# A start-up sequence written out for one step more, with a new order of work on every engine, in a 16-graph attention kernel

## The chip, the cores and the metric

The kernel runs on one core of a Trainium2 chip. The metric is the device time of one execution in microseconds (us). TensorE is called PE, VectorE DVE, ScalarE ACT, GpSimd POOL, and the queue that issues most plain loads and stores SP.

## What is computed

For 16 graphs of 512 nodes with 256 features each, two layers run one after the other, each with a residual and a layer norm:

```python
# layer 0: graph attention
h = x @ W_fc.T;  f1 = h @ a1;  f2 = h @ a2
scores = leaky_relu(f1[:, :, None] + f2[:, None, :], 0.2)
scores = where(adj == 0, -1e9, scores)
h_prime = softmax(scores, axis=2) @ x
x = layernorm(x + elu(h_prime))
# layer 1: similarity, adjacency, features
xn = x / sqrt(max(sum(x * x), 1e-12))
out = ((xn @ xn.T) @ adj) @ x
x = layernorm(x + out)
```

## The kernel before

One graph is one unit of work `g`; its 512 rows are four chunks `c` of 128 partitions, and the 256 features are two halves `d`. Nothing is planned at run time: each engine has one list of calls, written out by hand, and runs it strictly in that order. Semaphores tie the lists together. So the order inside each list, and nothing else, sets what waits for what.

A step on PE, in the names of the code: `transpose_prob(g, c)` (L1117) turns a softmax block; `attend(g, c)` (L1137 for graphs 0 and 1, L1140 to L1142 from graph 2 on, 12 matmuls a call) multiplies it with x; `make_z(g, c)` (L1170, L1171, 8 matmuls) multiplies the adjacency with the normalised xn; `transpose_xn(g, d)` (L1182); `make_w(g, d)` (L1200 to L1202, 12 matmuls); `make_out(g, c)` (L1214, 4 matmul records); `bcast_f2(g)` (L1106) spreads the column scores. Three PSUM banks `ps_l1` are used in turn by z, xnT, w and out; `bank_free` lets PE write a bank once the reader of the tile three places earlier is done.

ACT does, per graph: `make_mask` (L783), `lrelu` (L793), `softmax_exp` (L804), `probT_hi_part` (L813), `elu_exp` (L824), `elu_relu` (L830), `xn_hi_part` (L838), `scale_z` (L857), `copy_xnT` (L866), `copy_w` (L872) and `normalise2` (L890, four activations). DVE does `node_scores` (L433), `masked_f2` (L449), `negate_max`, `denominators`, `probT_lo_part` (L486), `residual` (L494), `row_moments` (L527, L531), `normalise` (L540), `z_lo_part` (L549), `residual2` (L560) and `row_moments2` (L590). POOL does `residual_sum` (L278), `shifted_moments` and `power` (L285 to L295), `norm`, `split_xn` (L311), `split_x` (L267), `shifted_moments2`, `power2` (L340), `shift2` (L347), and issues the loads `load_adj` (L259) and `load_x_hi` (L252). SP issues `load_x` and `store`.

The steps are skewed: step `i` of the loops attends graph `i`, makes z and w of graph `i - 1`, makes the output of graph `i - 2`, and prepares the softmax of graph `i + 1`. Each list has a head written out call by call, a loop `for i in range(3, B - 2)` with one steady order (B is 16), and a tail written out again. The lists in the head differ from the order of the loop, since the pipeline is filling.

Two chains matter later. For xn: `elu_relu(g, 3)` on ACT, `residual(g)` on DVE, `residual_sum(g)` on POOL, `row_moments(g)` on DVE, `shifted_moments(g)` and `power(g)` on POOL, `normalise(g)` on DVE, `xn_hi_part(g)` on ACT, `split_xn(g)` on POOL, then `make_z(g, 0)` on PE. For the output: `make_out(g, 0)` waits for `copy_xnT(g, 0)`, `copy_xnT(g, 1)`, `copy_w(g, 0)` and `copy_w(g, 1)`, all on ACT. And `attend(g, c)` for c of 2 or more waits for `elu_relu(g, c - 2)`, which frees its PSUM bank.

## Time and profile before

| | |
|---|---|
| median of 3 runs | 336.14 us (335.92 to 337.16) |
| the profiled execution | 337.11 us |
| its span, first to last instruction | 335.2 us |
| PE busy | 320.5 us (96%) |
| ACT busy | 291.2 us (87%) |
| DVE busy | 282.6 us (84%) |
| POOL busy | 206.2 us (62%) |
| mean granted TensorE clock | 0.991 of full speed |
| moved by DMA | 41.38 MB, mean 123 GB/s |

The profiled execution is 1.9 us longer than its span (what lies before the first and after the last instruction), and 0.97 us above the median of the runs. Busy time says how much of the span an engine worked; starts and ends in the rows are in us from the start of the span. Matmuls overlap in the pipeline, so one call's cost is read from start to start, not from the length of a row. A line beginning with an engine name in a list of waits tells who waited, for whom, for how long in all, how often, and the longest.

### The profile page before, as it was taken

Reading aid. Unit: us, or ns where it says so; the run is one execution under the profiler, and the core shown is the slowest. Engines: PE = TensorE matmul, PEld = TensorE weight load, DVE = VectorE, ACT = ScalarE, POOL = GpSimd, SP = SyncE. Lnnn points to the kernel's source line nnn. Section 1 sums busy time; section 2 is a strip of 40 time slices with the busy share of each in tenths; the row PEclk is TensorE's granted clock in tenths of the full one; section 3 lists DMA queues with packets and bytes.
Section 4 is the critical chain, followed back from the end, with each engine's and each line's share of the span. In section 5 each row is a group of like instructions: output and inputs, shape, how many; then the busy total and the mean of one; then the engine's idle time right before and its main releaser. Section 6 shows DMA issues by size and latency. Waiting matters only on the chain.

```text
span 335.2 us, 7276 instructions
## 1 busy us (share of the span) xinstructions
PE 320.5 (96%) x2376; PEld 301.4 (90%) x2376; DVE 282.6 (84%) x1000; ACT 291.2 (87%) x606; POOL 206.2 (62%) x236
## 2 busy tenths in 40 slices
PE   8998999997979999999999999999999999999992
PEld 5777999997979999999999999999999999998881
DVE  4899998897498989899898989899898988947635
ACT  4988889998399999999999999999999998993561
POOL 4044775856058576666858576666858576665623
PEclk9999999999899999999999999999999999999998
DMA  7774506215224554462554564553653551210121
GB/s 221 221 188 129 165 26 177 81 59 186 69 63 127 151 162 128 114 192 74 172 143 126 153 163 127 123 183 74 175 142 126 150 165 65 64 65 0 49 78 63
DMA packets 32964, 41.38 MB, mean 123 GB/s; under 512 B 1152, under 2 KB 24736, under 8 KB 32928
## 3 DMA queue, kind: packets, MB, share of 16 engines
q0 software_dynamic: 15888, 24.12, 26.5%
q1 hardware_dynamic: 16992, 16.81, 16.0%
q8 instruction: 19, 0.31, 0.4%
q14 instruction: 17, 0.14, 0.1%
q10 hardware_dynamic: 48, 0.00, 0.0%
HBM read 32.54 MB, written 8.39 MB: 122 GB/s over the span
## 4 chain that ended last, share of the span: by engine, by line
PE 86%; DVE 6%; ACT 4%; issue 2%; POOL 1%; POOLq 0%; DVEq 0%; ACTq 0%
PE ps_l L1214 16%; PE ps_l L1170 9%; PE ps_l L1171 8%; PE ps_h L1140 8%; PE ps_probT L1117 8%; PE ps_h L1141 8%; PE ps_h L1142 8%; PE ps_l L1200 4%; PE ps_l L1202 4%; PE ps_l L1201 4%; PE ps_l L1182 4%; PE ps_h L1137 3%; PE ps_f L1106 2%; DVE product L433 1%; PE ps_l L1197 1%
## 5 line engine op out<-in xcount | busy, mean ns | idle before, releaser
L1140 PE MATMUL ps_h<-x_hi,probT_hi 128*128 128x256 f32 x224 | 69.0, 308 | 0.7 <-issue 0.7
L1170 PE MATMUL ps_l<-xn_hi,adj_sb 128*128 128x256 f32 x256 | 63.9, 288 | 2.8 <-POOL xn_lo L311 1.7
L1214 PE MATMUL ps_l<-w_sb,xnT 128*128 128x256 f32 x256 | 63.1, 383 | 2.2 <-ACT xnT L866 1.9
L1141 PE MATMUL ps_h<-x_lo,probT_hi 128*128 128x256 f32 x224 | 63.0, 281 | 0.0
L1142 PE MATMUL ps_h<-x_hi,probT_lo 128*128 128x256 f32 x224 | 62.9, 281 | 0.0
L1171 PE MATMUL ps_l<-xn_lo,adj_sb 128*128 128x256 f32 x256 | 62.5, 283 | 0.0
L311 POOL TENSOR_TENSOR xn_lo<-xn,xn_hi 128x1024 fp32r<-128x1024 f32 x15 | 36.0, 2401 | 41.0 <-ACT xn_hi L838 41.0
L1170 PEld LDWEIGHTS ps_l<-xn_hi,adj_sb 128*128 128x128 f32 x256 | 48.9, 191 | 4.5 <-DVE y L560 2.7
L1214 PEld LDWEIGHTS ps_l<-w_sb,xnT 128*128 128x128 f32 x256 | 45.5, 190 | 8.0 <-ACT xnT L866 2.2
L1171 PEld LDWEIGHTS ps_l<-xn_lo,adj_sb 128*128 128x128 f32 x256 | 48.9, 191 | 0.0
L433 DVE CUSTOM_DVE_ANT_0 product<-x_sb,v_bcast 128x256 bf16<-128x256 f32 x128 | 47.1, 426 | 0.0
L804 ACT ACTIVATE prob<-score,neg_max 128x512 f32<-128x512 f32 x64 | 46.5, 728 | 0.2
L793 ACT ACTIVATE score<-score,f 128x512 f32<-128x512 f32 x64 | 44.4, 723 | 2.1 <-DVE row_max L449 2.1
L1140 PEld LDWEIGHTS ps_h<-x_hi,probT_hi 128*128 128x128 f32 x224 | 42.7, 191 | 3.8 <-DVE probT_lo L486 1.9
L449 DVE CUSTOM_DVE_ANT_0 score<-mask,ps_f 128x512 f32<-128x512 bf16 x64 | 41.3, 685 | 3.7 <-ACT mask L783 3.6
L1141 PEld LDWEIGHTS ps_h<-x_lo,probT_hi 128*128 128x128 f32 x224 | 42.7, 191 | 0.7
L278 POOL TENSOR_TENSOR y<-y,exp_h 128x1024 f32<-128x1024 f32 x15 | 36.1, 2408 | 11.1 <-DVE exp_h L494 10.8
L1142 PEld LDWEIGHTS ps_h<-x_hi,probT_lo 128*128 128x128 f32 x224 | 42.6, 190 | 0.0
L486 DVE TENSOR_TENSOR probT_lo<-ps_probT,probT_hi 128x512 fp32r<-128x512 f32 x56 | 36.9, 680 | 2.4 <-ACT probT_hi L813 2.4
L1117 PE MATMUL ps_probT<-ident,prob 128*128 128x128 f32 x256 | 38.0, 273 | 0.4 <-ACT prob L804 0.2
L560 DVE SCALAR_TENSOR_TENSOR y<-xn,nrm,ps_l 128x256 f32<-128x256 f32 x64 | 29.4, 477 | 9.8 <-PE ps_l L1214 9.5
L857 ACT ACTIVATE z_hi<-ps_l,nrm 128x256 fp32r<-128x256 f32 x60 | 28.3, 473 | 10.4 <-PE ps_l L1171 8.9
(82 smaller groups left out, 819.9 us busy)
## 6 DMA issues: line engine op xcount, KB each, us to landing
adj_sb<-adj POOLq DMA_DIRECT2D x15, 1024.0 KB, 5.9
x_sb<-x SPq DMA_DIRECT2D x16, 512.0 KB, 4.6
out<-o_sb SPq DMA_DIRECT2D x15, 512.0 KB, 3.2
x_hi<-x POOLq DMA_DIRECT2D x14, 512.0 KB, 4.1
adj_sb<-adj POOLq DMA_DIRECT2D x4, 256.0 KB, 4.8
out<-o_sb SPq DMA_DIRECT2D x4, 128.0 KB, 1.7
wfc<-w_fc SPq DMA_DIRECT2D x1, 32.0 KB, 2.0
attn_cols<-w_attn ACTq DMA_DIRECT2D x1, 0.2 KB, 1.7
```

Source lines behind the costliest of these rows:

```text
L433: last = nc.vector.tensor_tensor_reduce(out=product[:, k, c, :], in0=x_sb[n][:, c, :], in1=v_bcast[:, k, :], scale=1.0, scalar=0.0, op0=AL ...
L449: nc.vector.tensor_tensor_reduce(out=score[:, c, :], in0=mask[:, c, :], in1=ps_f2[:], scale=1.0, scalar=LOWEST, op0=ALU.add, op1=ALU.max, ...
L486: nc.vector.tensor_tensor(probT_lo[:, c, :], ps_probT[c % 2][:], probT_hi[:, c, :].bitcast(F32), ALU.subtract).then_inc(probT_ok, 1)
L793: nc.scalar.activation(score[:, c, :], score[:, c, :], ACT.Prelu, bias=f[n][:, 0, c:c + 1], scale=1.0, alpha=SLOPE).then_inc(lrelu_ok, 1)
L804: nc.scalar.activation(prob[:, c, :], score[:, c, :], ACT.Exp, bias=neg_max[n][:, c:c + 1], scale=1.0, accum_out=den[n][:, c:c + 1]).then_ ...
L1117: last = nc.tensor.transpose(ps_probT[c % 2][:, k * P:(k + 1) * P], prob[:, c, k * P:(k + 1) * P], ident[:])
L1140: nc.tensor.matmul(ps, probT_hi[:, c, blk], x_hi[n][:, k, :], start=(k == 0), stop=False)
L1141: nc.tensor.matmul(ps, probT_hi[:, c, blk], x_lo[n][:, k, :], start=False, stop=False)
L1142: last = nc.tensor.matmul(ps, probT_lo[:, c, blk], x_hi[n][:, k, :], start=False, stop=(k == NC - 1))
L1170: nc.tensor.matmul(ps, a, xn_hi[n][:, k, :], start=(k == 0), stop=False)
L1171: last = nc.tensor.matmul(ps, a, xn_lo[n][:, k, :], start=False, stop=(k == NC - 1))
L1214: last = nc.tensor.matmul(ps, xnT[:, d, c * P:(c + 1) * P], w_sb[:, d, :], start=(d == 0), stop=(d == DC - 1))
```

## The change

Every list gets one more step written out before its loop, and the loops start at 4 in place of 3. The body of the loops and the tails are not touched. Each call that was made before is made once again, so each engine has the same instructions in another order. Within the head the order is new on DVE, ACT, PE and POOL, from the first graph on, most of it by one to ten places; SP loads x of graph 5 before it stores graph 0, and POOL issues `load_x_hi` for graphs 3, 4 and 5 earlier. The diff, without the reordering of DVE's and ACT's lists for the first two graphs:

```diff
--- before.py
+++ after.py
@@ -221,8 +221,10 @@
             load_x(2)
             load_x(3)
             load_x(4)
+            load_x(5)
             store(0)
-            for i in range(3, B - 2):
+            store(1)
+            for i in range(4, B - 2):
                 load_x(i + 2)
                 store(i - 2)
             store(B - 4)
@@ -349,41 +351,52 @@
             load_adj(1)
             residual_sum_part(0)
             load_adj(2)
-            load_x_hi(2)
+            load_x_hi(3)
             residual_sum_part(1)
             residual_sum_part(2)
             residual_sum_part(3)
-            load_x_hi(3)
+            load_x_hi(2)
             shifted_moments(0)
             power(0)
             norm(0)
             residual_sum(1)
             load_adj(3)
+            load_x_hi(4)
             shifted_moments(1)
             power(1)
             norm(1)
             split_xn(1)
             split_x(2)
+            split_x(3)
+            load_adj(4)
             shifted_moments2(0)
-            split_x(3)
-            load_x_hi(4)
-            load_adj(4)
+            load_x_hi(5)
             power2(0)
+            shift2(0)
             residual_sum(2)
-            shift2(0)
             split_x(4)
             shifted_moments(2)
             power(2)
+            split_xn(2)
             norm(2)
-            split_xn(2)
             shifted_moments2(1)
             power2(1)
-            shift2(1)
             load_adj(5)
             residual_sum(3)
+            shift2(1)
+            split_x(5)
             shifted_moments(3)
             power(3)
-            for i in range(3, B - 2):
+            split_xn(3)
+            norm(3)
+            load_adj(6)
+            shifted_moments2(2)
+            residual_sum(4)
+            power2(2)
+            shift2(2)
+            shifted_moments(4)
+            power(4)
+            for i in range(4, B - 2):
                 norm(i)
                 split_xn(i)
                 load_x_hi(i + 2)
...
@@ -648,13 +661,13 @@
             row_moments(1)
             negate_max(2, 0)
             node_scores(3, 1)
+            negate_max(2, 1)
+            normalise(1)
             node_scores(3, 0)
-            normalise(1)
             residual2(0, 0)
-            negate_max(2, 1)
             probT_lo_part(2, 0)
+            probT_lo_part(2, 1)
             residual2(0, 1)
-            probT_lo_part(2, 1)
             residual2(0, 2)
             residual2(0, 3)
             denominators(2)
@@ -663,18 +676,43 @@
             masked_f2(3, 0)
             masked_f2(3, 1)
             masked_f2(3, 2)
-            masked_f2(3, 3)
+            z_lo_part(1, 1)
+            z_lo_part(1, 2)
+            negate_max(3, 0)
             probT_lo_part(2, 2)
             probT_lo_part(2, 3)
-            negate_max(3, 0)
+            node_scores(4, 0)
+            node_scores(4, 1)
+            masked_f2(3, 3)
+            z_lo_part(1, 3)
             negate_max(3, 1)
-            z_lo_part(1, 1)
-            z_lo_part(1, 2)
-            z_lo_part(1, 3)
-            node_scores(4, 1)
             residual(2)
             probT_lo_part(3, 0)
-            for i in range(3, B - 2):
+            probT_lo_part(3, 1)
+            row_moments(2)
+            denominators(3)
+            probT_lo_part(3, 2)
+            probT_lo_part(3, 3)
+            masked_f2(4, 0)
+            masked_f2(4, 1)
+            normalise(2)
+            negate_max(4, 0)
+            residual2(1, 0)
+            masked_f2(4, 2)
+            residual2(1, 1)
+            residual2(1, 2)
+            residual2(1, 3)
+            masked_f2(4, 3)
+            row_moments2(1)
+            z_lo_part(2, 0)
+            node_scores(5, 1)
+            negate_max(4, 1)
+            z_lo_part(2, 1)
+            z_lo_part(2, 2)
+            z_lo_part(2, 3)
+            residual(3)
+            probT_lo_part(4, 0)
+            for i in range(4, B - 2):
                 probT_lo_part(i, 1)
                 row_moments(i - 1)
                 denominators(i)
...
             lrelu(3, 1)
             lrelu(3, 2)
-            lrelu(3, 3)
             elu_exp(2, 0)
             elu_relu(2, 0)
-            scale_z(1, 2)
+            softmax_exp(3, 0)
             elu_exp(2, 1)
             elu_relu(2, 1)
+            softmax_exp(3, 1)
+            elu_exp(2, 2)
             scale_z(1, 3)
-            softmax_exp(3, 0)
-            elu_exp(2, 2)
             elu_relu(2, 2)
             elu_exp(2, 3)
             elu_relu(2, 3)
-            softmax_exp(3, 1)
+            lrelu(3, 3)
+            copy_xnT(1, 0)
             probT_hi_part(3, 0)
+            probT_hi_part(3, 1)
             softmax_exp(3, 2)
-            copy_xnT(1, 0)
-            probT_hi_part(3, 1)
-            copy_xnT(1, 1)
             softmax_exp(3, 3)
+            make_mask(4)
             probT_hi_part(3, 2)
+            probT_hi_part(3, 3)
             copy_w(1, 0)
             copy_w(1, 1)
+            copy_xnT(1, 1)
+            elu_exp(3, 0)
+            elu_relu(3, 0)
             normalise2(0)
-            probT_hi_part(3, 3)
-            elu_exp(3, 0)
-            make_mask(4)
-            elu_relu(3, 0)
+            xn_hi_part(2)
             elu_exp(3, 1)
-            xn_hi_part(2)
+            elu_relu(3, 1)
             lrelu(4, 0)
-            elu_relu(3, 1)
+            softmax_exp(4, 0)
+            elu_exp(3, 2)
             lrelu(4, 1)
             lrelu(4, 2)
-            lrelu(4, 3)
-            elu_exp(3, 2)
+            scale_z(2, 0)
             elu_relu(3, 2)
             elu_exp(3, 3)
-            scale_z(2, 0)
-            elu_relu(3, 3)
-            softmax_exp(4, 0)
             softmax_exp(4, 1)
             scale_z(2, 1)
             scale_z(2, 2)
             scale_z(2, 3)
+            elu_relu(3, 3)
+            softmax_exp(4, 2)
+            copy_xnT(2, 0)
+            lrelu(4, 3)
             probT_hi_part(4, 0)
             probT_hi_part(4, 1)
-            copy_xnT(2, 0)
-            softmax_exp(4, 2)
+            copy_w(2, 0)
             softmax_exp(4, 3)
-            normalise2(1)
-            copy_w(2, 0)
+            copy_xnT(2, 1)
             copy_w(2, 1)
             probT_hi_part(4, 2)
+            normalise2(1)
             probT_hi_part(4, 3)
-            copy_xnT(2, 1)
             elu_exp(4, 0)
             elu_relu(4, 0)
-            elu_exp(4, 1)
-            elu_relu(4, 1)
             make_mask(5)
             xn_hi_part(3)
             lrelu(5, 0)
+            elu_exp(4, 1)
+            elu_relu(4, 1)
             lrelu(5, 1)
+            lrelu(5, 2)
+            lrelu(5, 3)
             elu_exp(4, 2)
-            for i in range(3, B - 2):
+            elu_relu(4, 2)
+            elu_exp(4, 3)
+            elu_relu(4, 3)
+            softmax_exp(5, 0)
+            scale_z(3, 0)
+            softmax_exp(5, 1)
+            scale_z(3, 1)
+            softmax_exp(5, 2)
+            scale_z(3, 2)
+            scale_z(3, 3)
+            probT_hi_part(5, 0)
+            probT_hi_part(5, 1)
+            softmax_exp(5, 3)
+            copy_xnT(3, 0)
+            probT_hi_part(5, 2)
+            copy_xnT(3, 1)
+            copy_w(3, 0)
+            copy_w(3, 1)
+            probT_hi_part(5, 3)
+            normalise2(2)
+            elu_exp(5, 0)
+            make_mask(6)
+            xn_hi_part(4)
+            elu_relu(5, 0)
+            lrelu(6, 0)
+            elu_exp(5, 1)
+            elu_relu(5, 1)
+            elu_exp(5, 2)
+            lrelu(6, 1)
+            for i in range(4, B - 2):
                 elu_relu(i + 1, 2)
                 lrelu(i + 2, 2)
                 elu_exp(i + 1, 3)
...
@@ -1222,18 +1291,18 @@
             transpose_prob(0, 1)
             transpose_prob(0, 2)
             attend(0, 0)
+            transpose_prob(0, 3)
             attend(0, 1)
             bcast_f2(1)
-            transpose_prob(0, 3)
             attend(0, 2)
             attend(0, 3)
             transpose_prob(1, 0)
             transpose_prob(1, 1)
-            bcast_f2(2)
             attend(1, 0)
+            attend(1, 1)
             transpose_prob(1, 2)
             transpose_prob(1, 3)
-            attend(1, 1)
+            bcast_f2(2)
             attend(1, 2)
             attend(1, 3)
             make_z(0, 0)
@@ -1245,9 +1314,9 @@
             make_w(0, 0)
             make_w(0, 1)
             transpose_prob(2, 0)
+            transpose_prob(2, 1)
+            make_out(0, 0)
             bcast_f2(3)
-            make_out(0, 0)
-            transpose_prob(2, 1)
             make_out(0, 1)
             make_out(0, 2)
             make_out(0, 3)
@@ -1262,15 +1331,36 @@
             attend(2, 2)
             attend(2, 3)
             transpose_prob(3, 0)
+            transpose_prob(3, 1)
             transpose_xn(1, 0)
             make_w(1, 0)
-            transpose_prob(3, 1)
             transpose_xn(1, 1)
+            make_w(1, 1)
+            bcast_f2(4)
             transpose_prob(3, 2)
-            bcast_f2(4)
-            make_w(1, 1)
             transpose_prob(3, 3)
-            for i in range(3, B - 2):
+            attend(3, 0)
+            attend(3, 1)
+            make_out(1, 0)
+            attend(3, 2)
+            make_out(1, 1)
+            make_out(1, 2)
+            make_out(1, 3)
+            attend(3, 3)
+            make_z(2, 0)
+            make_z(2, 1)
+            make_z(2, 2)
+            make_z(2, 3)
+            transpose_prob(4, 0)
+            transpose_xn(2, 0)
+            transpose_xn(2, 1)
+            transpose_prob(4, 1)
+            make_w(2, 0)
+            make_w(2, 1)
+            transpose_prob(4, 2)
+            transpose_prob(4, 3)
+            bcast_f2(5)
+            for i in range(4, B - 2):
                 make_out(i - 2, 0)
                 attend(i, 0)
                 make_out(i - 2, 1)
```

## Rows read from the trace of the kernel before

**Rows 1.** Page, part 1: busy us, share of the span, instructions.

```profile
PE 320.5 (96%) x2376; PEld 301.4 (90%) x2376; DVE 282.6 (84%) x1000; ACT 291.2 (87%) x606; POOL 206.2 (62%) x236
```

**Rows 2.** Busy us by stretch: length, then PE, PEld, DVE, ACT, POOL; PE clock, DMA.

```profile
32.70:62.07 29.37, 29.35 (x224) 28.23 (x225) 25.93 (x89) 26.54 (x59) 19.76 (x18) 1.00 0.39 109
62.07:83.35 21.28, 19.34 (x149) 18.47 (x148) 18.95 (x72) 20.66 (x44) 13.12 (x16) 1.00 0.37 117
83.35:106.12 22.77, 20.96 (x148) 19.94 (x149) 16.37 (x60) 15.86 (x33) 10.70 (x12) 0.93 0.35 100
106.12:124.97 18.85, 18.85 (x151) 18.26 (x150) 17.25 (x65) 18.24 (x39) 13.25 (x15) 1.00 0.48 140
124.97:269.00 144.03, 144.03 (x1127) 139.31 (x1126) 132.55 (x483) 139.58 (x290) 101.06 (x109) 1.00 0.49 140
```

**Rows 3.** PE in order of time, both stalls: start, length, [idle before, releaser].

```profile
80.81 0.60 PE L1117 MATMUL ps_probT<-ident,prob 128*128 128x128 f32 x4
83.35 1.76 PE L1214 MATMUL ps_l<-w_sb,xnT 128*128 128x256 f32 x4 [1.94 <-ACT xnT L866]
...
95.97 0.35 PE L1170 MATMUL ps_l<-xn_hi,adj_sb 128*128 128x256 f32 x1 [1.69 <-POOL xn_lo L311]
```

**Rows 4.** ACT in order of time around the stalls.

```profile
79.22 2.08 ACT L890 ACTIVATE o_sb<-y,bias,scale 128x256 f32<-128x256 f32 x4
...
82.68 0.62 ACT L866 ACTIVATE xnT<-ps_l 128x512 f32<-128x512 f32 x1
87.52 0.47 ACT L824 ACTIVATE exp_h<-ps_h,rden 128x256 f32<-128x256 f32 x1 [4.22 <-PE ps_h L1142]
87.90 0.47 ACT L830 ACTIVATE y<-ps_h,rden 128x256 f32<-128x256 f32 x1
...
90.52 1.91 ACT L783 ACTIVATE mask<-adj_sb 128x2048 bf16<-128x2048 f32 x1
92.32 1.06 ACT L838 ACTIVATE xn_hi<-xn 128x1024 fp32r<-128x1024 f32 x1
```

**Rows 5.** Clock and busy us: the start, and between the two stalls.

```profile
12.00:32.70 20.70, 19.08 (x103) 15.71 (x101) 19.92 (x74) 18.69 (x41) 7.79 (x12) 1.00 0.63 165
...
83.35:87.12 3.77, 3.77 (x15) 3.46 (x16) 3.46 (x14) 0.00 (x0) 0.97 (x3) 0.55 0.63 186
```

**Rows 6.** DVE in order of time: `normalise(3)`, four instructions.

```profile
85.55 1.38 DVE L540 TENSOR_SCALAR xn<-y,mv,powers 128x256 f32<-128x256 f32 x4
```

**Rows 7.** POOL in order of time: graph 2's sum, graph 3's chain.

```profile
58.45 2.38 POOL L278 TENSOR_TENSOR y<-y,exp_h 128x1024 f32<-128x1024 f32 x1 [4.05 <-DVE exp_h L494]
...
81.51 0.23 POOL L285 TENSOR_SCALAR moments<-mv 128x4 f32<-128x4 f32 x1 [1.95 <-DVE mv L531]
...
82.16 1.67 POOL L295 TENSOR_TENSOR powers<-moments,minus_half 128x8 f32<-128x8 f32 x1
...
93.45 2.37 POOL L311 TENSOR_TENSOR xn_lo<-xn,xn_hi 128x1024 fp32r<-128x1024 f32 x1 [8.97 <-ACT xn_hi L838]
```

**Rows 8.** PE in order of time: matmuls of `make_out`, and the start of `make_z(4, 0)`.

```profile
43.15 2.76 PE L1214 MATMUL ps_l<-w_sb,xnT 128*128 128x256 f32 x12
...
115.26 0.28 PE L1170 MATMUL ps_l<-xn_hi,adj_sb 128*128 128x256 f32 x1
```

**Rows 9.** POOL and ACT by time in a steady step.

```profile
112.43 2.40 POOL L311 TENSOR_TENSOR xn_lo<-xn,xn_hi 128x1024 fp32r<-128x1024 f32 x1 [2.42 <-ACT xn_hi L838]
112.96 1.34 ACT L793 ACTIVATE score<-score,f 128x512 f32<-128x512 f32 x2
```

**Rows 10.** Groups by line, one steady step: count, busy us, mean ns.

```profile
L494 DVE SCALAR_TENSOR_TENSOR exp_h<-exp_h,x_sb 128x1024 f32<-128x1024 f32 x1 | 1.2, 1218 | 0.0
```

**Rows 11.** POOL, DVE and PE in order of time near the tail.

```profile
274.17 2.37 POOL L267 TENSOR_TENSOR x_lo<-x_sb,x_hi 128x1024 fp32r<-128x1024 f32 x1
275.84 0.99 DVE L433 CUSTOM_DVE_ANT_0 product<-x_sb,v_bcast 128x256 bf16<-128x256 f32 x1
276.64 0.36 PE L1140 MATMUL ps_h<-x_hi,probT_hi 128*128 128x256 f32 x1 [0.70 <-issue]
```

More of the change, by code:

```diff
@@ L613, in _ @@
             residual_part(0)
+            probT_lo_part(0, 3)
             masked_f2(1, 0)
@@ L616, in _ @@
             masked_f2(1, 2)
-            probT_lo_part(0, 3)
             negate_max(1, 0)
+            masked_f2(1, 3)
             node_scores(2, 1)
-            residual_part(1)
-            masked_f2(1, 3)
             probT_lo_part(1, 0)
             negate_max(1, 1)
+            residual_part(1)
             residual_part(2)
-            residual_part(3)
             probT_lo_part(1, 1)
             row_moments_part(0)
+            residual_part(3)
             row_moments_part(1)
@@ L632, in _ @@
             probT_lo_part(1, 2)
+            node_scores(2, 0)
             probT_lo_part(1, 3)
-            node_scores(2, 0)
             normalise_part(0)
@@ L905, in _ @@
             softmax_exp(0, 3)
-            make_mask(1)
             elu_exp(0, 0)
             elu_relu(0, 0)
+            make_mask(1)
             elu_exp(0, 1)
+            elu_relu(0, 1)
             lrelu(1, 0)
             lrelu(1, 1)
-            elu_relu(0, 1)
             elu_exp(0, 2)
-            elu_relu(0, 2)
             softmax_exp(1, 0)
             softmax_exp(1, 1)
+            elu_relu(0, 2)
+            lrelu(1, 2)
+            lrelu(1, 3)
             elu_exp(0, 3)
             elu_relu(0, 3)
-            lrelu(1, 2)
-            lrelu(1, 3)
             softmax_exp(1, 2)
@@ L924, in _ @@
             elu_relu(1, 0)
-            make_mask(2)
             elu_exp(1, 1)
             elu_relu(1, 1)
+            make_mask(2)
             elu_exp(1, 2)
@@ L930, in _ @@
             xn_hi_first(1)
+            xn_hi_first(2)
             elu_relu(1, 2)
-            xn_hi_first(2)
             xn_hi_first(3)
@@ L937, in _ @@
             scale_z(0, 1)
+            scale_z(0, 2)
             lrelu(2, 0)
-            scale_z(0, 2)
-            lrelu(2, 1)
             scale_z(0, 3)
             copy_xnT(0, 0)
+            lrelu(2, 1)
             lrelu(2, 2)
             copy_xnT(0, 1)
-            lrelu(2, 3)
             softmax_exp(2, 0)
@@ L950, in _ @@
             probT_hi_part(2, 0)
+            probT_hi_part(2, 1)
             xn_hi_part(1)
-            probT_hi_part(2, 1)
+            lrelu(2, 3)
             softmax_exp(2, 2)
@@ L956, in _ @@
             scale_z(1, 0)
+            scale_z(1, 1)
             probT_hi_part(2, 2)
             probT_hi_part(2, 3)
-            scale_z(1, 1)
             lrelu(3, 0)
+            scale_z(1, 2)
             lrelu(3, 1)
             lrelu(3, 2)
-            lrelu(3, 3)
             elu_exp(2, 0)
             elu_relu(2, 0)
-            scale_z(1, 2)
+            softmax_exp(3, 0)
             elu_exp(2, 1)
             elu_relu(2, 1)
+            softmax_exp(3, 1)
+            elu_exp(2, 2)
             scale_z(1, 3)
-            softmax_exp(3, 0)
-            elu_exp(2, 2)
             elu_relu(2, 2)
```

## The prediction

> **What bounds the kernel now.** I first read the page's busy shares: PE works 96% of the span [rows 1], and the change leaves PE's instructions as they are. So a new order can only remove time in which PE waits or runs slowly. Where that time lies is read from the table of busy time by stretch [rows 2]. A steady step of the loop takes 18.85 us and PE is busy in all of it (106.12 to 124.97); the 144.03 us behind it are 7.64 such steps, with no loss either. The 29.37 us ahead of 62.07 have none. The reader should see that two steps stand out: the loop's first (i = 3) takes 21.28 us and its second (i = 4) 22.77 us. They are 2.43 and 3.92 us over a steady step, together **6.35 us**. Nearly everything that this change can win is there.
>
> Then PE in order of time [rows 3]. `make_out(2, 0)` starts at 83.35 after 1.94 us of idle time, released by ACT's xnT copy; `make_z(3, 0)` starts at 95.97 after 1.69 us, released by POOL's xn_lo. ACT's rows tell why [rows 4]. The first stall: ACT runs `normalise2(1)` (2.08 us from 79.22), the w copies, two probT_hi, and only at 82.68 `copy_xnT(2, 1)`, for which PE stands still. The second: ACT is then idle for 4.22 us, since its next call is `elu_exp(4, 0)`, and `xn_hi_part(3)` stands behind `elu_exp(4, 1)` and the mask (90.52, 1.91 us). It starts at 92.32, although its input was there at 86.93 [rows 6]; POOL's split takes 93.45 to 95.82 [rows 7] and PE waits for it. Between both, the granted clock fell: 0.55 on average from 83.35 to 87.12 [rows 5], which is TensorE at its lower level, 1.2 GHz, nearly all the while.
>
> The 6.35 us are thus 1.94 + 1.69 of idle time; about 1.7 for the clock (from 83.35 `make_out(2, 0)` and `attend(4, 0)` are 4 records of 0.22 us and 12 matmuls of 0.12 us, 2.3 us at full speed, and they took 4.0, since `elu_exp(4, 0)` begins at 87.52 only [rows 4]); 1.0 us are small waits at hand-overs.
>
> **The change, part by part.** I follow the new lists forward in time, from where PE stands in the trace of before. Costs, start to start: `attend` 12 matmuls of 0.117 = 1.40 us, `make_z` 8 of 0.12 = 0.96, `make_out` 4 of 0.216 = 0.86 (12 take 2.76 with the last one's tail [rows 8]), a group of four transposes 0.44, `make_w` 1.41. Four attend, make_z and make_out, two make_w and seven groups of transposes give 18.8 us, the steady step of rows 2. ACT: elu_exp and elu_relu 0.37 each [rows 4], lrelu 0.61 (two in 1.34 with one tail [rows 9]), softmax_exp 0.71, probT_hi and xnT 0.49, xn_hi 1.0, mask 1.85, normalise2 2.0.
>
> *To 32.7 us.* From 12.0 on DVE is busy 19.92 of 20.70 us [rows 5], and `split_xn_part(3)`, for which `make_z(0, 0)` waits, has the same DVE calls before it in both orders. Moving the transposes ahead of `attend(0, 1)` and `bcast_f2(2)` behind `attend(1, 1)` closes PE's small gaps, but PE then waits for DVE anyway: worth 0, within 0.3 us either way.
>
> *32.7 to 62 us.* PE has no loss here [rows 2] and none to win. A late link would cost. POOL issues `load_x_hi(4)` ahead of `shifted_moments(1)`, 0.8 us of POOL's time; the wait of `load_adj(3)` ahead of it sets POOL to 38.0, so graph 1's moments move by 0.2 us at most. `load_x_hi(5)` now waits for `attend(2, 3)` (about 56.2), with power2(0), shift2(0) and residual_sum(2) queued behind it. POOL idled 4.05 us until 58.45 there [rows 7] and the load and power2 need 1.9. SP's `load_x(5)` past `store(0)` starts when `residual(2)` ends (58.5) rather than behind the store; nothing needs it later. I follow 0.
>
> *The new step 3.* It starts at 61.95. ACT has `copy_w(1, ·)` and `copy_xnT(1, 1)` done at 64.3, so `make_out(1, 0)`, now behind two attends, starts at 64.8 unhindered. `normalise2(0)` runs 65.0 to 67.0, power(2) ends at 65.9, normalise(2) at 67.3, xn_hi(2) at 68.3, split_xn(2) at 70.8; PE reaches `make_z(2, 0)` at 71.05. ACT then does `copy_xnT(2, 1)` at 79.5 and `copy_w(2, 1)` at 80.0, **both ahead of `normalise2(1)`**, so `make_out(2, 0)` starts when PE comes to it, at 80.8. The first stall goes (2.5 us before 83.35), and with no long idle time the clock should not fall.
>
> *Step 4.* `residual(3)` 76.0 to 77.2 (1.22 us [rows 10]), residual_sum(3) 2.41 to 79.65, row moments 1.95 later by POOL's idle time in rows 7; POOL spends that time on `split_x(5)`, new here, until 82.3; moments 0.65 and power 1.7 to 84.85; normalise 1.38 to 86.2. ACT reaches `xn_hi_part(3)` behind the mask at 85.9, so it waits for xn and runs 86.2 to 87.2; POOL splits until 89.6. PE comes to `make_z(3, 0)` at 80.8 + 4 x 0.86 + 4 x 1.40 = 89.85. The second stall goes, by a margin of 0.2 us; before, the same split ended at 95.82.
>
> What is late next: `elu_relu(4, 1)` stands behind xn_hi(3) and `lrelu(5, 0)`, ends at 88.6 and holds `attend(4, 3)`, due at 88.4: +0.25. `z_lo_part(3, 0)` holds `make_z(3, 3)`: +0.3. `copy_w(3, 1)` holds `make_out(3, 0)`: +0.1. Sum of **new waits 0.65 us**. Step 5 then begins at about 100.2 in place of 106.12, with ACT as far ahead of PE as it was in a steady step. There ACT is busy 18.24 of 18.85 us [rows 2], so it keeps up but wins back little.
>
> **Sum**: 6.35 - 0.65 = 5.7 us. From the profiled execution, 337.11 - 5.7 = 331.4 us. The median is 0.97 us lower: 336.14 - 5.7 = 330.4. Whether the timed runs hold the stretch of slow clock I can't see; if none does, 1.7 us of the gain don't exist and the time is 336.14 - 4.0 = 332.1. I take 331.0 us: the full sum, less 0.6 us for links whose margin is 0.2 us or less. Bounds: all 6.35 us come back and the head wins another 0.3: 329.5; only the first idle wait goes: 336.14 - 1.9 = 334.2.
>
> The Trainium skill ("TensorE: Matmul & The Clock Gate", part 1) says that a busy engine is what releases the slow clock, and that how many matmuls run slow varies from run to run of one kernel. The trace agrees as far as one execution can: the clock fell with the first idle stretch and not with the second. By that rule the 1.7 us may be in some runs of before and not in others, the case of 332.1.
>
> **The rivals.** *The clock's share isn't there* (absent in the timed runs of before, or it falls elsewhere after): 4.0 us of gain, 332.1. For: one execution shows it. Against: it follows directly on the idle stretch.
>
> *One link is late.* xn_lo(3) has a margin of 0.2 us over a chain of eight hand-overs, and my times carry an error of some tenths. Then PE waits anew, up to the 1.69 us of rows 3, and may lose clock as well: 336.14 - 5.7 + 1.7 (+ 1.7) = 332.1 to 333.8.
>
> *The stalls move only.* The loop starts with another phase and the waits come back in step 5 or 6: between 335 and 337. For: ACT has 0.6 us of slack in a step. Against: before, the steps were at 18.85 us right after a loss of 3.92, so the order heals quickly.
>
> *Slower, by a wait in every step.* DVE's node_scores instruction starts at 275.84 [rows 11], during POOL's split_x (274.17 to 276.54), and takes 0.99 us where its kind takes 0.42; PE idles 0.70 us at 276.64. In the steady step the two just miss each other (both follow the end of residual_sum: row moments, rden and one probT_lo on DVE, shift2 and 2.4 us of split_x on POOL). If the new entry turned that miss into a hit in each of 10 steps at 0.57 to 0.70 us, it would cost 5.7 to 7.0 us and give 336 to 337.4; it decides from 0.57 us a step, and from 0.74 a step the kernel is slower by over 0.5%. Against: the distance of both is set by durations of the unchanged loop, not by the entry. The Trainium skill ("SBUF — State Buffer", "two separate sides") says the same as a rule: a DVE operation with two SBUF inputs and a GpSimd one that reads SBUF lock each other out for a whole instruction. The row agrees (0.99 against 0.42); by that rule `node_scores(5, 0)`, at 82.15 beside a split_x until 82.25, loses 0.1 us on DVE, and PE none.
>
> **How the numbers follow.** The sum as worked out, 330 to 332: 0.56. The clock's share absent: 0.14. A late link, to 334: 0.15. Stalls moved only: 0.10. A wait in every step or another slip: 0.05. About 0.5% (1.7 us) is what a measurement can tell from no change. Faster by more takes the first three, 0.85; within it 0.09; slower 0.06. The range 329.6 to 334.3 takes in the sum, its bounds and the first two rivals.
>
> **What would show it.** Right: the list of PE's waits holds neither xnT (L866) nor xn_lo of L311 above 0.5 us between 60 and 110; granted clock 1.00 throughout that stretch; step 5's `make_out(3, 0)` near 100; `xn_hi_part(3)` starts near 86 and `normalise2(1)` behind the w copies. The loop's steps keep 18.85 us. Wrong: a wait of `make_z(3, 0)` for xn_lo, a low clock elsewhere, PE idle 0.3 us or more in each step, or `make_z(0, 0)` later than 33.

## The result, and the profile after

| | before | after |
|---|---|---|
| median of 4 runs | 336.22 us (335.92 to 337.16) | 332.85 us (332.77 to 332.90) |
| the profiled execution | 337.11 us | 332.77 us |
| its span | 335.2 us | 330.8 us |
| mean granted clock | 0.991 | 0.997 |

The ratio of the times is 0.9887 (95% interval 0.9865 to 0.9909), and the quotient of the two medians 0.9900: the new head makes the kernel 1.0 to 1.1% faster. It is inside the predicted range and on the predicted side, 1.85 us slower than the predicted 331.0. It is outside the 330 to 332 us that I gave the chance of 0.56. All ratios and medians below leave out two slow runs of the kernel before, of 459 and 534 us.

The page of the changed kernel, part 1 (busy us, share of the span, instructions), which answers to [rows 1]:

```profile
PE 319.3 (97%) x2376; PEld 299.7 (91%) x2376; DVE 282.0 (85%) x1000; ACT 291.0 (88%) x606; POOL 206.9 (63%) x236
```

All counts are those of before. So nothing but the order has changed. The table by stretch of the changed kernel, columns as in [rows 2] (length, busy PE, PEld, DVE, ACT, POOL, granted clock, DMA), is cut where a step starts (step 3 begins with `attend(3, 0)` here and with `make_out(1, 0)` before, the others with `make_out(i - 2, 0)` in both; a step holds the same calls):

```profile
32.70:62.36 29.66, 29.26 (x225) 28.28 (x225) 25.89 (x95) 26.88 (x56) 20.51 (x19) 1.00 0.52 141
62.36:82.10 19.74, 19.53 (x151) 18.35 (x150) 17.14 (x58) 18.35 (x43) 13.15 (x15) 1.00 0.26 84
82.10:101.44 19.34, 19.16 (x150) 18.46 (x149) 17.32 (x64) 18.22 (x39) 11.20 (x13) 1.00 0.38 108
101.44:120.63 19.19, 19.02 (x151) 18.27 (x149) 17.86 (x67) 18.24 (x39) 12.52 (x15) 1.00 0.47 138
120.63:139.49 18.86, 18.86 (x151) 18.27 (x149) 17.25 (x65) 18.22 (x39) 13.27 (x15) 1.00 0.49 139
139.49:264.63 125.14, 125.14 (x978) 120.99 (x977) 115.17 (x420) 121.25 (x252) 87.87 (x95) 1.00 0.49 140
```

Steps 3 and 4 took 21.28 and 22.77 us before [rows 2]; they take 19.74 and 19.34 now, and the clock column says 1.00 where it said 0.93. From step 6 on a step is 18.86 us, the 18.85 of before. This gives the whole account. Before, 6.35 us were lost over steady steps. After, 0.89 + 0.49 + 0.34 = 1.72 us are lost in steps 3 to 5, and step 3 starts 0.29 us later (62.36 in place of 62.07). 6.35 - 1.72 - 0.29 = 4.34 us, which is the difference of the two profiled executions (337.11 - 332.77). From `make_out(5, 0)` to the end each call is 4.34 us earlier than before, and nothing comes back later.

The first five lines in the list of PE's waits of the changed kernel (who, for whom: us in all, times, longest):

```profile
PE ps_l L1156 <- DVE warm L430: 1.2, 1, 1.2
PE ps_h L1209 <- issue: 0.7, 1, 0.7
PE ps_l L1239 <- DVE xn_lo L529: 0.7, 1, 0.7
PE ps_probT L1186 <- ACT prob L842: 0.6, 2, 0.4
PE ps_h L1209 <- ACT y L868: 0.4, 2, 0.2
```

Neither the wait for xnT (1.94 us) nor the one for POOL's xn_lo (1.69 us) of [rows 3] is left. ACT in order of time shows the moved calls (start, length, line, operation); it answers to [rows 4]:

```profile
80.83 0.62 ACT L904 ACTIVATE xnT<-ps_l 128x512 f32<-128x512 f32 x1
81.31 0.42 ACT L910 ACTIVATE w_sb<-ps_l 128x256 f32<-128x256 f32 x1
82.05 2.12 ACT L928 ACTIVATE o_sb<-y,bias,scale 128x256 f32<-128x256 f32 x4
...
87.52 1.06 ACT L876 ACTIVATE xn_hi<-xn 128x1024 fp32r<-128x1024 f32 x1 [0.30 <-DVE xn L553]
```

The xnT copy now runs at 80.83, ahead of the four activations of `normalise2(1)`, and `xn_hi_part(3)` at 87.52, not 92.32; it now waits 0.30 us for its input, where before the input waited 5.4 us for it. PE in order of time of the changed kernel, at the places of the two stalls:

```profile
82.10 1.03 PE L1283 MATMUL ps_l<-w_sb,xnT 128*128 128x256 f32 x4
...
90.11 0.35 PE L1209 MATMUL ps_h<-x_hi,probT_hi 128*128 128x256 f32 x1 [0.18 <-ACT y L868]
91.59 0.28 PE L1239 MATMUL ps_l<-xn_hi,adj_sb 128*128 128x256 f32 x1
```

`make_out(2, 0)` (82.10) and `make_z(3, 0)` (91.59) carry no idle time. The row of `make_out(2, 0)` is 1.03 us long, against 1.76 in the kernel before [rows 3], where the lower clock began within it.

### The profile page after: what moved, and what is told of

It reads as the page before. It is cut to its first block, busy times and chain, and to the rows that moved or that the text cites. A ratio compares the mean times of both kernels' runs of the same rounds, so it can differ in the third digit from the quotient of the medians.

```text
span 330.8 us, 7276 instructions
## 1 busy us (share of the span) xinstructions
PE 319.3 (97%) x2376; PEld 299.7 (91%) x2376; DVE 282.0 (85%) x1000; ACT 291.0 (88%) x606; POOL 206.9 (63%) x236
## 4 chain that ended last, share of the span: by engine, by line
PE 82%; DVE 8%; POOL 4%; issue 3%; ACT 1%; POOLq 0%; DVEq 0%
PE ps_l L1283 14%; PE ps_l L1239 9%; PE ps_l L1240 9%; PE ps_h L1209 8%; PE ps_h L1210 7%; PE ps_h L1211 7%; PE ps_probT L1186 7%; PE ps_l L1269 4%; PE ps_l L1271 4%; PE ps_l L1270 4%; PE ps_l L1251 3%; DVE product L446 2%; PE ps_h L1206 2%; PE ps_f L1175 1%; POOL y L280 1%
## 5 line engine op out<-in xcount | busy, mean ns | idle before, releaser
L1209 PE MATMUL ps_h<-x_hi,probT_hi 128*128 128x256 f32 x224 | 68.3, 305 | 1.2 <-issue 0.7
L1283 PE MATMUL ps_l<-w_sb,xnT 128*128 128x256 f32 x256 | 62.3, 380 | 0.2
L1269 PE MATMUL ps_l<-xn_hi,z_hi 128*128 128x256 f32 x120 | 35.8, 298 | 0.2 <-DVE z_lo L562 0.2
```

The source lines that it names most:

```text
L1209: nc.tensor.matmul(ps, probT_hi[:, c, blk], x_hi[n][:, k, :], start=(k == 0), stop=False)
L1269: nc.tensor.matmul(ps, z_hi[:, k, blk], xn_hi[n][:, k, :], start=(k == 0), stop=False)
L1283: last = nc.tensor.matmul(ps, xnT[:, d, c * P:(c + 1) * P], w_sb[:, d, :], start=(d == 0), stop=(d == DC - 1))
```

## The experiments

Two theories are told apart. The first: two places in ACT's list, those of `normalise2(1)` and `xn_hi_part(3)`, are the whole of it, and the rest of the new head is worth nothing or costs a little. The second: the gain needs the new head as a whole, and the one step more that it writes out.

All experiments come in three sets, each with its own runs of the kernel before. Those runs fall into two groups: 20 of the 29 took 337.0 to 337.4 us with a mean clock of 0.991 to 0.993, nine took 335.4 to 336.2 us with 0.996 to 0.998. The median of before is 337.1 us in each of the three sets. A ratio takes in the runs of both groups and is therefore nearer to 1 than the quotient of the medians. The changed kernel itself ran only beside the result, so a difference to its 332.85 us goes from one set to another; the faster group of before moves between sets by up to 0.8 us, and differences of a few tenths are therefore read from traces as well.

One more thing has to be known for reading two traces against each other. At the start PE runs at its lower level, and the clock rises at another moment in each execution: 8.3 us in the changed kernel, 8.6 in the kernel before, 9.3 to 11.0 in the experiments (there the warm-up matmuls, until then 0.21 us apart, come 0.11 us apart). A later rise can make `make_z(0, 0)` later, and everything behind it.

**The two edits of ACT's list, each alone and together, in the kernel before.** The first edit moves `normalise2(1)` and `copy_xnT(2, 1)`:

```diff
-            normalise2(1)
             copy_w(2, 0)
+            copy_xnT(2, 1)
             copy_w(2, 1)
             probT_hi_part(4, 2)
+            normalise2(1)
             probT_hi_part(4, 3)
-            copy_xnT(2, 1)
```

> The kernel before with one edit on ACT: normalise2(1) moves behind copy_xnT(2, 1) and copy_w(2, 1), as in the changed head. Theory A (the first stall is made by the place of that one call): make_out(2, 0) starts at about 81.3 in place of 83.35, its wait for xnT is gone, the granted clock stays 1.00 behind it, and the wait of make_z(3, 0) for xn_lo stays at 1 to 2 us, as its order is untouched. 2.1 us less from the wait, and up to 1.7 us more where the slow clock was there: 332.3 to 334.0. Rival B (ACT is the bound of the whole head, so that the order of single calls only moves the wait): the wait comes back on the next ACT product, w or probT_lo, and the time stays within 0.5 us of 336.2.

Measured: 333.68 us (333.37 to 334.03), ratio 0.9911 (0.9882 to 0.9941). The second edit moves the mask and `xn_hi_part(3)`:

```diff
-            elu_exp(4, 1)
-            elu_relu(4, 1)
             make_mask(5)
             xn_hi_part(3)
+            elu_exp(4, 1)
+            elu_relu(4, 1)
             lrelu(5, 0)
```

> The kernel before with the other edit on ACT: make_mask(5) and xn_hi_part(3) move ahead of elu_exp(4, 1). Theory A: the first stall stays at 1.9 us, with the slow clock behind it (mean clock 0.991 in the profile); make_z(3, 0) has no wait above 0.3 us: 336.2 - 1.7 = 334.5. Rival B: attend(4, 3) then waits for elu_relu(4, 1) as long as make_z did before, 336.

Measured: 333.81 us (333.35 to 334.08), ratio 0.9913 (0.9884 to 0.9943). Then both edits at once:

> The kernel before with both edits on ACT and nothing else: no new step written out, DVE, POOL, PE and SP as before. Theory A (two misplaced calls on ACT are the whole gain, and the rest of the new head costs 0.4 us up to make_z(0, 0), 0.6 us in step 3 and 0.7 us in steps 4 and 5): both stalls and the slow clock are gone, 330.8 to 332.2, faster than the changed kernel's 332.85. Rival C (the new head must be balanced as a whole): one of the stalls stays or moves, 333 or more.

Measured: 331.82 us (331.74 to 332.29), ratio 0.9858 (0.9833 to 0.9884), which is 1.0 us *less* than the changed kernel (0.8 between the profiled executions, 331.95 and 332.77). The first line of PE's waits that concerns this stretch, of the kernel with the first edit, and then of the kernel with the second:

```profile
PE ps_l L1170 <- POOL xn_lo L311: 1.7, 1, 1.7
```

```profile
PE ps_l L1214 <- ACT xnT L866: 1.9, 1, 1.9
```

Each edit takes away one wait and leaves the other. With both, ACT in order of time reads as in the changed kernel, though nothing else in the head is new:

```profile
79.82 0.62 ACT L866 ACTIVATE xnT<-ps_l 128x512 f32<-128x512 f32 x1
81.35 0.38 ACT L872 ACTIVATE w_sb<-ps_l 128x256 f32<-128x256 f32 x1 [0.91 <-PE ps_l L1202]
82.11 2.07 ACT L890 ACTIVATE o_sb<-y,bias,scale 128x256 f32<-128x256 f32 x4
...
87.10 1.06 ACT L838 ACTIVATE xn_hi<-xn 128x1024 fp32r<-128x1024 f32 x1
```

So the first theory holds: two edits, four moved calls in all, with the loop still starting at 3, give all of the gain and 1.0 us besides. The one step more that is written out is not what gains. Whether the first edit needs both of its calls is not tested in this kernel; the next experiment tests `normalise2(1)` alone in the changed one.

The gains of the edits alone add up to more than that of both. The steps tell why. Step 4 is 22.77 us in the kernel before and 21.07 with the first edit, both with the wait for xn_lo: 1.70 us is what the low clock costs there. With the second edit alone step 4 is 18.90 us, and with both it is 19.43: since PE is no longer 2 us late, small waits come up that its lateness had covered, one of them 0.2 us at `make_z(3, 3)` for DVE's z_lo.

The clock did something that I had not expected. The kernel with the second edit keeps PE's 1.9 us of idle time, and its clock does not fall behind it. This is its table by stretch, behind the idle time; [rows 5] has 0.55 for the same place:

```profile
83.77:87.50 3.73, 3.73 (x25) 3.52 (x26) 3.65 (x15) 1.16 (x3) 0.96 (x3) 1.00 0.63 187
```

The mean clock was 0.994 to 0.996 in all four of its runs.

**One call put back in the changed kernel.**

```diff
             copy_w(2, 0)
             softmax_exp(4, 3)
+            normalise2(1)
             copy_xnT(2, 1)
             copy_w(2, 1)
             probT_hi_part(4, 2)
-            normalise2(1)
```

> The changed kernel with normalise2(1) put back ahead of copy_xnT(2, 1) and copy_w(2, 1). Theory A: make_out(2, 0) waits some 1.9 us again and what follows is late with it: 334.5 to 335; where the slow clock follows on an idle stretch of this length, the profile shows it near 85 and the time is up to 1.7 us more, 336.5. If the clock stays at 1.00, the idle stretch alone doesn't bring the slow clock. Rival B: ACT's order doesn't matter, 332.9.

Measured: 334.64 us (334.22 to 334.98, 8 runs), ratio 0.9937 (0.9917 to 0.9958): 1.8 us slower than the changed kernel. PE in order of time of this kernel at `make_out(2, 0)`:

```profile
83.85 0.70 PE L1283 MATMUL ps_l<-w_sb,xnT 128*128 128x256 f32 x2 [1.57 <-ACT xnT L904]
```

The first stall is back, and with it 1.75 us on the path (83.85 in place of 82.10). Step 4 takes 0.30 us of it back (19.04 in place of 19.34), so that the profiled executions differ by 1.56 us. The mean clock stayed at 0.995 to 0.998 in all eight runs. So in the changed kernel the place of this one call is worth 1.6 to 1.8 us, all of it idle time and none of it clock.

**What costs the changed kernel 0.9 us in step 3.** Its POOL and DVE in order of time:

```profile
57.03 0.79 POOL L254 DMA_DIRECT2D x_hi<-x  x1 [4.07 <-PE ps_h L1211]
57.85 1.92 POOL L342 TENSOR_TENSOR scale<-ve,minus_half 128x4 f32<-128x4 f32 x1
...
60.01 2.38 POOL L280 TENSOR_TENSOR y<-y,exp_h 128x1024 f32<-128x1024 f32 x1
```

```profile
57.64 1.23 DVE L507 SCALAR_TENSOR_TENSOR exp_h<-exp_h,x_sb 128x1024 f32<-128x1024 f32 x1
```

POOL waits 4.07 us for PE's last read of the buffer that `load_x_hi(5)` fills. Then `power2(0)`, an operation on only four elements per partition, takes 1.92 us (as in all four traces with this order on POOL); it took 1.05 in the kernel before. It starts 0.21 us after DVE's `residual(2)`, which reads two operands of SBUF until 58.87. `residual_sum(2)`, whose input is there at 58.87, starts at 60.01, and the chain to `make_z(2, 0)` is as much later. That a load was issued just before is not the reason, for in the kernel before `power2(0)` followed a load without a gap and took 1.05 us:

```profile
52.58 0.75 POOL L259 DMA_DIRECT2D adj_sb<-adj  x1
53.34 1.05 POOL L340 TENSOR_TENSOR scale<-ve,minus_half 128x4 f32<-128x4 f32 x1
```

I made two kernels to see whether the order on POOL can cure it. One sets the load behind the sum:

```diff
-            load_x_hi(5)
             power2(0)
             shift2(0)
             residual_sum(2)
+            load_x_hi(5)
             split_x(4)
```

> The changed kernel with one edit on POOL: load_x_hi(5) moves behind residual_sum(2). In the changed kernel it waits for attend(2, 3) until 57.03, then power2(0) takes 1.92 us and residual_sum(2) starts at 60.01, 1.15 us after its input. Theory A (that is what makes xn of graph 2 late and costs PE 0.55 us in step 3): residual_sum(2) starts at 58.9, the waits of attend(3, 3) and make_z(2, 0) are gone, 332.85 - 0.5 = 332.3. Rival B (ACT is late in step 3 whatever POOL does): attend(3, 3) still waits for elu_relu(3, 1), and the time stays at 332.8.

Measured: 332.97 us (332.67 to 333.24, 5 runs), ratio 0.9886 (0.9867 to 0.9905): no gain. `power2(0)` was back at 1.04 us, but the load's 0.85 us now stood between the sum and graph 2's moments. Its clock rose at 10.3 us, so its rows are read from `make_z(0, 0)` on (33.51 here, 33.10 in the changed kernel): `power(2)` starts 32.22 us behind it in place of 32.39, only 0.17 us better. The other kernel sets `power2(0)` and `shift2(0)` ahead of the load:

```diff
-            load_x_hi(5)
             power2(0)
             shift2(0)
+            load_x_hi(5)
             residual_sum(2)
```

> The changed kernel with power2(0) and shift2(0) ahead of load_x_hi(5), the load still ahead of residual_sum(2). Theory A (power2(0) took 1.92 us in place of 1.05 because DVE's residual(2), 57.64 to 58.86, ran beside it, so that the two engines held each other up): power2(0) now runs near 53 and takes 1.0 to 1.1 us, the load is issued at 57.0 to 57.8, and residual_sum(2) starts at 58.9. Rival B (it was slow for another reason, such as the load issued just before it): the operation behind the load, now residual_sum(2), takes 0.8 us more than its 2.4.

Measured, in one execution: 332.05 us (the last kernel below has the same edit, in five runs). Its POOL in order of time:

```profile
53.05 1.04 POOL L342 TENSOR_TENSOR scale<-ve,minus_half 128x4 f32<-128x4 f32 x1
57.08 0.85 POOL L254 DMA_DIRECT2D x_hi<-x  x1 [2.67 <-PE ps_h L1211]
59.00 2.40 POOL L280 TENSOR_TENSOR y<-y,exp_h 128x1024 f32<-128x1024 f32 x1 [1.08 <-DVE exp_h L507]
```

The power runs inside POOL's wait and takes 1.04 us, the sum starts 1.01 us earlier (59.00 against 60.01), `power(2)` 1.0 earlier, `make_out(2, 0)` 0.78 earlier (81.32 against 82.10), and the end comes 0.7 us earlier (`make_out(15, 3)` at 322.84 against 323.56). Both have `make_z(0, 0)` at 33.1. Step 3 takes 18.92 us in place of 19.74: this one place on POOL is nearly all of its loss. The load is in the same place on the clock as in the changed kernel, beside `residual(2)`, and costs nothing there; behind the sum, in the first kernel of this pair, its 0.85 us stand on the chain.

**The early order, up to `make_z(0, 0)`.** In the changed kernel the lists of DVE, ACT and PE for the first two graphs are put back as they were before (the same calls):

> The changed kernel with the old order of the first graphs, up to make_z(0, 0), on PE, ACT and DVE. Theory A (there the new order loses 0.38 us, since the mask of graph 1 is made behind elu_exp(0, 0), masked_f2(1, 0) starts at 18.70 in place of 17.85, and DVE bounds that stretch): make_z(0, 0) at 32.7 in place of 33.1, 332.85 - 0.4 = 332.5. Rival B (the later start is absorbed by waits behind it): 332.8.

Measured: 332.42 us (332.39 to 333.13), ratio 0.9876 (0.9856 to 0.9896), 0.43 us under the changed kernel. ACT in order of time, of this kernel and then of the changed one:

```profile
14.46 1.90 ACT L821 ACTIVATE mask<-adj_sb 128x2048 bf16<-128x2048 f32 x1
16.35 0.47 ACT L862 ACTIVATE exp_h<-ps_h,rden 128x256 f32<-128x256 f32 x1
```

```profile
15.59 0.47 ACT L862 ACTIVATE exp_h<-ps_h,rden 128x256 f32<-128x256 f32 x1 [1.05 <-PE ps_h L1206]
15.96 0.47 ACT L868 ACTIVATE y<-ps_h,rden 128x256 f32<-128x256 f32 x1
16.32 1.91 ACT L821 ACTIVATE mask<-adj_sb 128x2048 bf16<-128x2048 f32 x1
```

The new list puts graph 1's mask behind an `elu_exp` for which ACT waits 1.05 us, so the mask is 1.86 us later, and with it DVE's `masked_f2(1, 0)` (18.70 in place of 17.85) ahead of `split_xn_part(3)`. The price is best read from two kernels whose clock rose at the same time at the start (10.3 us in both): `make_z(0, 0)` starts at 33.11 with the old order (second edit above) and at 33.51 with the new one (load behind the sum). So the new early order costs 0.40 us. The 0.43 us between the medians says the same, but goes from one set to another.

**The new waits of attend in steps 4 and 5.**

```diff
-            lrelu(5, 0)
             elu_exp(4, 1)
             elu_relu(4, 1)
+            lrelu(5, 0)
             lrelu(5, 1)
...
             elu_exp(5, 0)
+            elu_relu(5, 0)
             make_mask(6)
             xn_hi_part(4)
-            elu_relu(5, 0)
```

> The changed kernel with two edits on ACT: lrelu(5, 0) behind elu_relu(4, 1), and elu_relu(5, 0) ahead of make_mask(6). Theory A: attend(4, 3), 0.34 us late, and attend(5, 2), 0.35 to 0.5 us late, start when PE comes to them, 332.85 - 0.7 = 332.1. Rival B (xn_hi(4) is then late by the 0.36 us and POOL's split holds make_z(4, 0)): half of it or less, 332.5 or more.

Measured: 332.74 us (332.47 to 333.15), ratio 0.9881 (0.9862 to 0.9901), 0.11 under the changed kernel, which is inside the scatter of both. `attend(4, 3)` starts at 89.76 in place of 90.11 and `attend(5, 2)` at 107.53 in place of 108.05, 0.35 and 0.52 us earlier; `make_z(4, 0)` at 110.65 in place of 110.92 keeps 0.27 of it, and by step 6 (`make_out(4, 0)`, 120.43 against 120.63) 0.20 is left. So these waits are worth about 0.2 us: the rest is lost again at the links behind them, such as a new wait of 0.17 us at `make_z(3, 3)` in this trace.

**One call in the tail.** The 0.7 us "issue" wait of `attend(B - 2, 0)` stands in all kernels so far. To the kernel with both ACT edits I added, in PE's tail:

```diff
+            make_out(B - 4, 0)
             attend(B - 2, 0)
             attend(B - 2, 1)
-            make_out(B - 4, 0)
             make_out(B - 4, 1)
```

> The kernel before with the two ACT edits of e4_both, and in the tail make_out(B - 4, 0) ahead of attend(B - 2, 0). In every trace so far PE idles 0.70 us ahead of attend(14, 0), near 276 us in the kernel before. Theory T (it waits for POOL's split_x(14), which ends 0.1 us before attend(14, 0) starts; in the loop a make_out lies ahead of attend and covers it): the wait is gone, 331.82 - 0.8 = 331.0. Rival U (PE waits for DVE, whose node_scores instruction is held up to 0.99 us there): the wait moves to another call of PE and the time stays at 331.8.

Measured: 330.98 us (330.81 to 331.12), ratio 0.9831 (0.9807 to 0.9855), 0.84 us less than without it. Its PE in order of time, and POOL's row that counts:

```profile
270.28 0.60 PE L1117 MATMUL ps_probT<-ident,prob 128*128 128x128 f32 x4
270.71 1.03 PE L1214 MATMUL ps_l<-w_sb,xnT 128*128 128x256 f32 x4
271.58 0.36 PE L1140 MATMUL ps_h<-x_hi,probT_hi 128*128 128x256 f32 x1
```

```profile
269.11 2.37 POOL L267 TENSOR_TENSOR x_lo<-x_sb,x_hi 128x1024 fp32r<-128x1024 f32 x1
```

POOL's `split_x(14)` ends at 271.48 and `attend(14, 0)` follows at 271.58; `make_out` fills the time. In [rows 11] it is the same: the split ends at 276.54 and attend starts at 276.64. The distance is 0.10 to 0.11 us in all twelve traces, and in the code `attend(g, 0)` waits for x_lo. So the wait was for x_lo, which the profile did not name.

**All of it together.** The changed kernel with the old early order, with the power ahead of the load, and with the tail edit:

> The changed kernel with what the runs so far showed to cost it: the old order up to make_z(0, 0) on PE, ACT and DVE (0.4 us), power2(0) and shift2(0) ahead of load_x_hi(5) (0.8 us), and the tail edit of e10_both_tail (0.8 us). If the three are independent: 332.85 - 2.0 = 330.9, the same as e10_both_tail within 0.3 us, and then the new head is worth no more than two moved calls. If the new head is better once mended: 330.5 or less. If the gains overlap: 331.5 or more.

Measured: 330.79 us (330.77 to 331.22, 5 runs), ratio 0.9828 (0.9804 to 0.9853). From the parts 332.85 - 0.43 - 0.80 - 0.84 = 330.78 us: they add up. And it ends with the kernel before plus three edits (330.98, in the same set), within the scatter of both. So a repaired new head is worth the same as the old head with two edits in ACT's list, and the change's own step more is worth nothing that shows here.

## Why the prediction was right, and where it was wrong

**What bounds the kernel, and where the loss lies: right.** The steps kept 18.85 us, the loss was in two steps, and removing two waits removed most of it. `make_out(2, 0)` and `make_z(3, 0)` lost both idle times, and each edit alone brings 3.3 to 3.4 us against the median of before (first two experiments). The two together bring 5.3 (337.1 - 331.8), less than their sum. In the runs of either edit alone the low clock is gone as well, and that share, 1.7 us, is only to be had once.

**"To 32.7 us: worth 0, within 0.3": wrong by size.** It costs 0.40 us, and `make_z(0, 0)` at 33.10 is one of the signs of being wrong that I had set (later than 33). I checked that DVE's calls ahead of `split_xn_part(3)` were the same, but not that what feeds them, ACT's mask, had moved behind a wait for PE. Against the trace of before, `make_z(0, 0)` is 0.38 us later (33.10 against 32.72), 0.29 of which is left when step 3 starts.

**"32.7 to 62 us: 0": wrong, the largest miss.** I took 1.9 us for the load and the power out of POOL's 4.05 us of idle time [rows 7], but not the moment at which they can begin. The load waits for `attend(2, 3)`, so both fall at the end of that idle time, where `residual(2)` runs on DVE. They took 0.79 + 1.92 = 2.71 us, and the sum started 1.1 us after its input. In this kernel the small power operation started under DVE's residual takes 1.92 us, and in the head and the loop away from it 1.04 to 1.09. The prediction quoted the rule for this case (the Trainium skill, "SBUF — State Buffer", "SBUF: two separate sides") and applied it to `node_scores(5, 0)` alone. By that rule my estimate for `power2(0)` would have been up to the 1.0 us by which it overlaps `residual(2)`, near the 0.87 measured.

**Step 3 without loss: wrong by 0.89 us, as a consequence.** The forecast had `power(2)` ending at 65.9, `xn_hi_part(2)` starting at 67.3, and the split ending at 70.8. Measured: 67.16, 68.60 and 72.14, 1.3 us late each. `make_z(2, 0)` starts at 72.28, right behind the split, and `attend(3, 3)` at 70.53, because its `elu_relu(3, 1)` stands behind `xn_hi_part(2)` on ACT. In the kernel with the power ahead of the load, where the `make_out(1, 3)` before it starts at the same 69.30, they start at 71.57 and 69.98. So `attend(3, 3)` loses 0.55 us and `make_z(2, 0)` 0.16 us more.

**Step 4's margin of 0.2 us at `make_z(3, 0)`: held.** The split of graph 3 ends at 91.04, not 89.6, but PE comes at 91.59, not 89.85, because it was itself late. The chain of eight hand-overs moved with PE's own delay (in the kernel with the power ahead of the load the split ends 0.76 us and PE comes 0.78 us earlier), and the rival of a late link at this place did not come true. A late link came one graph earlier, at xn(2), where I had seen no risk; the median of 332.85 us lies in the band that this rival was given, and not in that of the sum.

**The new waits, 0.65 us: right in size, not in place.** Steps 4 and 5 lose 0.49 + 0.34 = 0.83 us. The wait of `attend(4, 3)` for `elu_relu(4, 1)` came (0.34 us, forecast 0.25), those of `make_z(3, 3)` and `make_out(3, 0)` did not, and step 5 has one that I had not looked for, of `attend(5, 2)` for `elu_relu(5, 0)` behind the mask and xn_hi (0.52 us late, of which the step keeps 0.34).

Together, for the profiled executions: 5.7 forecast, less 0.29 at the start, less 0.89 in step 3, less 0.83 - 0.65 = 0.18 in steps 4 and 5, is 4.34, the gain between the two profiled executions.

**The clock's share: right as a mechanism that may be absent, wrong as to the value I took.** I subtracted the full sum from a median of which I did not know whether it holds the slow stretch. Of the four runs of before that stand with the result, three (335.92 to 336.30) are like the runs without it in the later sets. So the medians differ by 3.37 us and the profiled executions by 4.34; the 0.97 between them is the 0.89 by which before's profiled execution is over that median, and 0.08 on the side of after. Had the sum of waits been right, the median would have been near the rival's 332.1. My allowance of 0.6 us covered part of it: 1.36 (the waits) + 0.97 (the clock) - 0.6, and 0.1 between the medians of before, is the miss of 1.85 us. The two groups of before lie 1.0 to 1.7 us apart in the three sets, and in step 4 the low clock costs 1.70 us (22.77 against 21.07, first edit); I had estimated 1.7. Against a median of before from the later sets (337.1) the same kernel gains 4.2 us.

**"Slower, by a wait in every step": didn't come, and the row behind it was misread.** The steps kept their length. PE's 0.70 us in [rows 11] is not owed to DVE's node_scores but to POOL's split_x itself (tail experiment). The stretched node_scores, 0.99 us from 275.84, ended at 276.83 and PE started at 276.64: it cost PE nothing.

What stays open: why the clock falls in most runs of before and in none of the kernels with one stall left. I can only say that the idle stretch alone doesn't decide it. Where the clock falls is seen in one execution of before only; for the others the mean clock and the time stand in for it.

## What to carry to other kernels

Before you rewrite a schedule, look for the one or two calls behind which the waiting one stands, and move these first: here two edits in one list gave 5.3 us, and a new head, 90 lines longer, gave 4.2. When a call goes into an idle stretch, take the time at which it *can start* and what runs on the neighbour engine at that time, not the length of the stretch. And when you subtract a gain read from one execution from a median, ask which part of it may not be in the median's runs; a granted clock that differs between them is such a part.

## What the runs showed of the hardware that I had not expected

- A POOL power operation on 128 x 4 elements took 1.92 us when it started 0.21 us into a DVE operation with two SBUF inputs of 1.23 us (four traces), and 1.04 to 1.09 us in the head and the loop otherwise; so an operation's size doesn't protect it. The Trainium skill ("SBUF — State Buffer", "SBUF: two separate sides") has the two lock each other out for a whole instruction, and these rows agree. One place in the tail does not: there the same kind of power is already running when DVE's residual starts (283.19 to 284.23 and 284.00 to 285.22 in the changed kernel). They overlap by 0.23 us, and neither is longer than elsewhere, in this trace or in the eleven others.
- The granted clock does not fall with an idle stretch of PE as such. In the profiled execution of before it falls at 83.71 us, 0.36 us after PE has begun again behind 1.94 us of idle time, and 20 of the 29 later runs have that execution's time and mean clock. The other nine, of the same kernel, have 0.996 to 0.998. With 1.9 us left (4 runs) or 1.57 (8 runs) at the same call the mean clock was never under 0.994.
- The moment at which the clock rises at the start, 8.3 to 11.0 us in twelve profiled executions, moves `make_z(0, 0)` with unchanged code. With the new order it starts at 33.10 to 33.12 for a rise between 8.3 and 9.5, and at 33.51 for one at 10.3; with the old order at 32.72 for a rise at 8.6, and at 33.04 to 33.11 for one at 10.1 to 10.3. So a difference of 0.4 us between two profiles has to be read between executions with the same rise.
